# A planned MoE, recurrence and MoE kernel: row normalisation moved from VectorE to GpSimd between its scatters, the pauses taken out, first groups of 4, 4 and 8 units

## What is computed

```python
x = x + 0.5 * ffn(layernorm(x))      # 8 experts, 128 -> 512 -> 128, relu squared; each token uses the expert of its largest router logit
x = x + rnn(layernorm(x))            # h = tanh(Wi x_t + bi + bh + Wh h), 512 steps, all 16 sequences at once
x = x + 0.5 * ffn(layernorm(x))      # the same experts again
```

## Time and profile before

| what | value |
|---|---|
| median of 3 executions | 612.68 us (606.79 to 624.44) |
| the profiled execution | 603.88 us, span 602.0 us |
| TensorE busy | 551.4 us (92%) |
| VectorE busy | 412.8 us (69%) |
| GpSimd busy | 423.5 us (70%), of which 187 pauses 116.0 us |
| ScalarE busy | 315.4 us (52%) |
| indirect DMAs of GpSimd | 64 + 64 scatters, 64 gathers, 71 puts, each 984 to 988 ns on average |
| normalisations on VectorE | 192 of 128x128, 65.1 us in all |

### The profile page before, as it was taken

The page is one execution under the profiler, slowest core; times in us unless marked ns, Lnnn a source line. Parts: engine busy times, 40 slices in busy tenths (PEclk is TensorE's granted clock), DMA queues, the critical chain, the costliest instruction groups (busy, mean ns, idle before and its releaser), DMA issues.

```text
span 602.0 us, 16237 instructions
## 1 busy us (share of the span) xinstructions
PE 551.4 (92%) x4714; PEld 533.7 (89%) x4714; DVE 412.8 (69%) x1507; ACT 315.4 (52%) x1089; POOL 423.5 (70%) x520
## 2 busy tenths in 40 slices
PE   7799798997999989999999999998999999869991
PEld 6798698897999989999999999997889999658991
DVE  5789867886667878657876774577546466665661
ACT  2133165464666546666666666654346666425660
POOL 2699497789995778978874987838849638664552
PEclk9889999998999999999999999999999999998997
DMA  5977432221222223322321532101152301435310
GB/s 184 296 273 289 109 105 81 79 78 59 78 80 69 66 82 97 93 68 63 98 81 49 132 111 77 39 27 68 45 144 76 84 20 69 139 115 151 101 37 1
DMA packets 54163, 58.89 MB, mean 98 GB/s; under 512 B 8999, under 2 KB 42034, under 8 KB 54080
## 3 DMA queue, kind: packets, MB, share of 16 engines
q1 hardware_dynamic: 44064, 36.68, 21.0%
q0 software_dynamic: 9440, 21.06, 10.8%
q10 hardware_dynamic: 576, 0.13, 0.1%
HBM read 27.67 MB, written 30.62 MB: 97 GB/s over the span
## 4 chain that ended last, share of the span: by engine, by line
PE 74%; DVE 11%; issue 7%; DMA 2%; SPq 1%; ACT 1%; another core or an unknown queue 1%; ACTq 0%; POOLq 0%; DVEq 0%
PE yp L1687 23%; PE hp L1677 20%; PE z L1697 11%; PE mT L1583 4%; PE lg L1627 3%; PE xTp L1666 3%; PE hp L1702 3%; DMA hsT<-in_L_attn_x_dram 2%; PE z L1647 2%; PE yp L1707 2%; DVE pay L1238 2%; DVE r_sb L1361 2%; PE hp L1616 1%; SPq L1012 1%
## 5 line engine op out<-in xcount | busy, mean ns | idle before, releaser
L1687 PE MATMUL yp<-projT,s_sb 128*128 x1248 | 198.3, 291 | 11.6 <-ACT s_sb L1495 5.9
L1677 PE MATMUL hp<-xT_sb,w_sb 128*128 128x128 f32 x1248 | 193.2, 286 | 2.0 <-DVE xT_sb L1355 1.3
L1687 PEld LDWEIGHTS yp<-projT,s_sb 128*128 128x128 f32 x1248 | 161.3, 194 | 14.6 <-issue 14.2
L1466 ACT ACTIVATE hsT<-z 128x16 f32<-128x16 f32 x512 | 93.5, 183 | 147.5 <-PE z L1697 102.7
L1677 PEld LDWEIGHTS hp<-xT_sb,w_sb 128*128 128x128 f32 x1248 | 161.7, 193 | 3.1 <-DVE xT_sb L1355 1.4
L1697 PEld LDWEIGHTS z<-hsT,wT 128*128 128x128 f32 x1024 | 154.0, 190 | 8.9 <-ACT hsT L1466 3.0
L1697 PE MATMUL z<-hsT,wT 128*128 128x16 f32 x1024 | 158.0, 230 | 1.4 <-ACT hsT L1466 1.2
L1495 ACT ACTIVATE s_sb<-r_sb 128x256 f32<-128x256 f32 (+1 forms) x252 | 115.7, 461 | 74.5 <-issue 51.8
L1361 DVE TENSOR_SCALAR r_sb<-hp 128x512 f32<-128x512 f32 x156 | 106.9, 686 | 66.6 <-PE hp L1677 55.9
L1152 POOL MEMSET idle<- 128x600 f32 x187 | 116.0, 620 | 0.2
L1189 POOL DMA_INDIRECT out_dram<-y_sb,xs_sb x71 | 70.1, 988 | 61.7 <-DVE y_sb L1368 34.9
(11 more groups left out here) (132 smaller groups left out, 564.3 us busy)
## 6 DMA issues: line engine op xcount, KB each, us to landing
xs_sb<-xs_dram SPq DMA_DIRECT2D x71, 129.0 KB
xs_sb<-xy_dram SPq DMA_DIRECT2D x85, 64.0 KB
xy_dram<-y_sb SPq DMA_DIRECT2D x85, 64.0 KB
xy_dram<-zeros SPq DMA_DIRECT2D x10, 512.0 KB, 6.0
hsT<-in_L_attn_x_dram SPq DMA_DIRECT2D x16, 256.0 KB
hsT<-n_L_ffn_expert_proj_dram SPq DMA_DIRECT2D x2, 1024.0 KB
fc_sb<-in_L_ffn_expert_fc_dram SPq DMA_DIRECT2D x1, 2048.0 KB
out_dram<-y_sb,xs_sb POOLq DMA_INDIRECT x71
```

Of the source, the lines that this page charges most:

```text
L1466: act.activation(state(t), z_step(t), ACT.Tanh).then_inc(s_h, 1)
L1677: mm = pe.matmul(hp[:, g % 2, h * P:(h + 1) * P], w_sb[:, g % 2, h * P:(h + 1) * P], xT_sb[:, g % 2, :], start=True, stop=True)
L1687: mm = pe.matmul(yp[:, 0:D], s_sb[:, g % 2, h, :], projT[:, bass.ds(offsets[g] + h * D, D)], start=(h == 0), stop=(h == HC - 1))
```

## The change

The normalisation of the two expert layers goes from VectorE to GpSimd. There it stands row tile by row tile between the scatters: the row tile j+1 is normalised ahead of the scatter of row tile j. The normalisation ahead of the recurrence stays on VectorE. The pauses are gone everywhere. The first layer's groups are 4, 4 and 8 units instead of 5, 3 and 8, the second layer's 4, 3, 2, 3, 2, 1, 1 instead of 3, 2, 2, 3, 2, 2, 1, 1, and the weights of the planner are others. Two of the first four units are loaded by ScalarE's DMA queue instead of SyncE's. The lists padded per expert are 23, 23 and 39 tiles, 85 as before. In the new plan GpSimd also takes the root of the second group in the middle of the first group's scatters, after nine of sixteen. And the gathers of unit 0 stand after four scatters of the third group, with the other early gathers mixed among these scatters; before, 31 of the 32 scatters of the third group stood in one row between the gathers of unit 2 and those of unit 3.

```diff
-FIRST = [5, 3, 8]
-STEP = [1, 3, 1]
-MIDDLE = [1, 1, 1, 1, 1, 1, 1, 1, 1, 1, 3, 3]
-SECOND = [3, 2, 2, 3, 2, 2, 1, 1]
+FIRST = [4, 4, 8]
+STEP = [1, 2, 1]
+MIDDLE = [1, 1, 1, 1, 1, 1, 2, 1, 1, 1, 3, 1, 1]
+SECOND = [4, 3, 2, 3, 2, 1, 1]
...
-REST = 600
+REST = 0
+PACE = 1.75
...
-PR = {'proj': -38.387, 'lat1': 30.338, 'lat2': 69.811, 'lat3': -18.484, 'last': 24.985,
+PR = {'proj': 82.557, 'lat1': 204.589, 'lat2': 80.915, 'lat3': -54.818, 'last': -288.677,
...
-AHEAD = [4, 5, 7]
+AHEAD = [3, 6, 7]
...
-    ROW, LAND, WINDOW = 1.27 + REST / 900, 2.2, 3.413
+    ROW, LAND, WINDOW = PACE if REST else 1.35, 2.2, 3.413
+    NORM = 0.45
...
     def normalising(r):
         n = range(r.J // 4)
-        return [("stats", r, i) for i in n] + [("root", r)] + [("norm", r, i) for i in n]
+        return [("stats", r, i) for i in n] + [("root", r)]
...
+            if what == "scatter" and p[1][2] + 1 < key.J:
+                pool_order.append(("norm", key, p[1][2] + 1))
+                start += NORM
+            while REST and drained > start + PR["burst"]:
+                pool_order.append(("rest",))
+                start += REST / 1250
+            pool_order.append(p[1])
+            pool_free, drained = start + 1.27, max(drained, start) + PACE
...
+        def by_act(u):
+
+            return u < FIRST[0] and u % 2 == 1
...
+            def normalise_row(r, j):
+
+                n, w = r.n0 + j, int(r.second)
+                if j == 0:
+                    pool.wait_ge(s_root, root_no["root", r.index])
+                pool.tensor_scalar(pay[:, n, XN:XN + D], row_in(w, n), mv[:, w, n, 0:1], rstd[:, w, n:n + 1],
+                                   ALU.subtract, ALU.mult).then_inc(s_row, 1)
+
             rests = [0]
...
-                if j % 4 == 0:
-                    pool.wait_ge(s_norm, 4 * norm_no["norm", r.index, j // 4])
+                pool.wait_ge(s_row, row_no[r.index, j])
...
-            def normalise(what, c, i):
-                w = 2 if what == "mnorm" else int(c.second)
-                dve.wait_ge(s_root, root_no["mroot" if what == "mnorm" else "root", c.index])
-                for n in range(c.n0 + 4 * i, c.n0 + 4 * i + 4):
-                    dve.tensor_scalar(pay[:, n, XN:XN + D], row_in(w, n), mv[:, w, n, 0:1], rstd[:, w, n:n + 1],
+            def normalise(m, i):
+                dve.wait_ge(s_root, root_no["mroot", m.index])
+                for n in range(m.n0 + 4 * i, m.n0 + 4 * i + 4):
+                    dve.tensor_scalar(pay[:, n, XN:XN + D], row_in(2, n), mv[:, 2, n, 0:1], rstd[:, 2, n:n + 1],
                                       ALU.subtract, ALU.mult).then_inc(s_norm, 1)
...
+            for u in range(min(FIRST[0], NU // 2)):
+                if by_act(u):
+                    act.dma_start(raw(u), x[:, u * UNIT:(u + 1) * UNIT, :].rearrange("b (th j) d -> th b (j d)", j=UR)
+                                  ).then_inc(s_in[u], 16)
```

More of the change, by code:

```diff
@@ L136, in first_in @@
         else:
-            at += {"rows": 1.1, "proj": 4.0, "fc": 8.0}[what[0]]
+            at += {"rows": 1.3, "proj": 4.0, "fc": 8.0}[what[0]]
         arrive[what] = at + 2.0
@@ L232, in urgency @@
         what = job[1][0][0]
-        return 16.0 - pe + PR["proj"] if what == "proj" else spare(job[0]) + (what in ("stats", "root", "norm")) * PR["late"]
+        return 16.0 - pe + PR["proj"] if what == "proj" else spare(job[0]) + (what in ("stats", "root")) * PR["late"]
     def pool_urgency(p):
@@ L757, in plan @@
             r = p[1] if len(p) > 1 else None
-            if p[0] == "place" or p[0] == "norm" and p[2] == r.J // 4 - 1:
-                placed, normed = ("place", r), ("norm", r, r.J // 4 - 1)
-                if placed in ev and normed in ev and r not in sorted_out:
-                    sorted_out.add(r)
-                    for j in range(r.J):
-                        pool_wait.append((max(ev[placed], ev["norm", r, j // 4], 0.0 if r.second else ev.get(("clean", r.index), 0.0)),
-                                          ("scatter", r, j)))
+            if p[0] == "place":
+                for j in range(r.J):
+                    pool_wait.append((max(ev[p], 0.0 if r.second else ev.get(("clean", r.index), 0.0)), ("scatter", r, j)))
             if p[0] == "list" and p[2] == 0 and r.last:
@@ L1073, in _ @@
                 if what[0] == "rows":
-                    rows_in(what[1])
+                    if not by_act(what[1]):
+                        rows_in(what[1])
                 elif what[0] == "zero":
@@ L1418, in side @@
                     statistics(*piece)
-                elif what in ("norm", "mnorm"):
-                    normalise(*piece)
+                elif what == "mnorm":
+                    normalise(*piece[1:])
                 elif what == "pick":
```

57 lines of the change are left out of this document (30 added, 27 removed).

## The result

The changed kernel takes 698.66 us (median of four runs, 691.60 to 706.73); the kernel before, on the same chip, takes 609.85 us. The ratio is 1.143, with a 95% interval of 1.133 to 1.153: clearly slower, where 588 us and 4.1% faster were predicted, and far above the range of 574 to 612 us. The profiled execution takes 691.87 us, its span is 689.8 us.

What follows compares the result with a forecast made beforehand. Bound taken: start 69.8 us, TensorE's work 494.4, holes 26.4, tail 11.4. Start -11.4, work -11.3 and holes -2 turn 603.9 into 579.2 us profiled, 588 us as a median (-4.1%), range 574 to 612 us.

Steps and rivals of the forecast that it cites:

- The pauses: GpSimd: 187 pauses of 0.61 us go, indirect DMAs follow one another in 1.27 us; their lack was priced at nothing.
- indirect DMAs that take longer than 0.97 us: Sign named as what would make all of the forecast wrong, if they do so once they follow closely.
- The normalisation: One row tile on GpSimd: taken as 0.45 us, between 0.29 and 0.55, giving a scatter spacing of 1.59 us (1.43 to 1.69).
- 20 us of slack: Third group: GpSimd's last early scatter ends near 162 us, while TensorE wants the group's first tile near 185 us.
- The start: Up to the first expert product: 58.4 us instead of 69.8, so -11.4 us, between -15 and -6.
- The rival of the start: The start gains nothing, by slow normalisation or a long wait at the root: 601 us as a median; chance 0.17.
- TensorE's work: From the first expert product on: 64 filler records go (13.3 us), the third group's rank adds 2.05 us; -11.3 us.
- The holes: TensorE's idle time after the first expert product: -2 us, between -8 and +12, as VectorE no longer normalises the third group.
- The rival of the dense order: Late gathers and scatters make TensorE stand still, then run at half clock; five holes give 623 us median; chance 0.13.
- The port lock: GpSimd's normalisations delay VectorE through shared ports, 6.3 us on the chain: 594 us as a median; chance 0.12.
- the sum: Whole kernel: 603.9 - 11.4 - 11.3 - 2 = 579.2 us profiled, times 1.0146 for the median.

Runs made afterwards that it cites:

- e6: The changed kernel, its order word for word, with 121 pauses of 0.62 us ahead of gathers and output transfers directly behind another indirect transfer: ratio 1.034.
- e5: The kernel before, its order word for word and VectorE normalising as before, with only GpSimd's pauses left out: 828 us, 36% slower.
- e1: The changed kernel, same order, with GpSimd normalising only 32 of a row's 128 columns: only about 10 us came back.
- e9: The changed kernel's order with pauses put in and GpSimd normalising only 32 of 128 columns: 590.8 us, 3.7% under the kernel before.
- e11: The changed kernel without pauses, its gathers and indirect transfers to the output moving 64 instead of 128 columns a row: the changed kernel's ratio.
- e14: The changed kernel's order with pauses ahead of gathers only, transfers to the output following each other without one: ratio 1.040.

## Why the prediction was wrong, step by step

**The pauses: the step that failed.** "So I price the lack of pauses at nothing". In the order of the change they are worth 10.9 points of the ratio (e6), near 66 us, in the old one 36% (e5). The step rested on one row, the scatter at 519.60 us that kept its 0.96 us without pauses. The row is right and shows the wrong thing: the transfer isn't slower, the engines that wait for TensorE's signals are. And the sign was there in the kernel before, on the other engines beside this very row. GpSimd issues bare transfers 1.27 us apart from 517.06 us on; these are VectorE's rows, and the stretches behind the second (columns as above):

```profile
524.30 0.69 DVE L1361 TENSOR_SCALAR r_sb<-hp 128x512 f32<-128x512 f32 x1 [2.64 <-remote]
...
540.10 0.29 DVE L1368 SCALAR_TENSOR_TENSOR y_sb<-yp,xs_sb 128x128 f32<-128x128 f32 x1 [3.40 <-remote]
```
```profile
539.00:543.00 4.00, 1.59 (x12) 1.15 (x10) 1.53 (x6) 0.91 (x2) 2.03 (x3) 1.00 0.35 118
543.00:547.00 4.00, 3.99 (x18) 3.50 (x19) 2.03 (x5) 1.79 (x3) 0.97 (x1) 0.57 0.59 133
```

Seven of the eight signals that come over 0.8 us late in the kernel before lie between 520 and 544 us, where GpSimd doesn't pause. What I had named as the proof against me, "indirect DMAs that take longer than 0.97 us", never came: bare gathers take 0.94 to 0.95 us in the stretch shown.

**The normalisation: mis-sized.** 0.82 us measured, 0.45 taken, and 0.55 the upper end. The extrapolation from 4 and 32 columns used an operation with an immediate in place of the two 128x1 operands; e1 gives 0.50 us at 32 columns with two operands of 128x1, so 0.0033 us a column and 0.39 us before the first. With the scatter's 1.07 us the spacing became 2.1 to 2.3 us, above the 1.69 us I had as the worst. With the pauses in place this is worth 36.5 us (e6 to e9, medians); in the profiled executions 19.6 of 33.1 us are idle time of TensorE. "20 us of slack" for them were not there.

**The start: half right.** The first scatter was to start at 20.7 us and starts at 20.73. No wait stands at the root (2.4 us taken), its 2.96 us are as said. But the last scatter of the first group starts at 56.55 us instead of 50.9: the fifteen spacings took some 7.7 us more than forecast, and the wait that didn't come gave 2.4 back. And the first expert product at 63.4 instead of 58.4: -6.4 us, where -11.4 was predicted and -6 was the end of the range. The rival of the start put its limit at 0.91 us for a normalisation, and 0.82 us plus the 0.10 us by which the scatter is dearer come to it; that the start still gains is owed to the wait that stayed away.

**TensorE's work: right in kind, and more than forecast.** -11.3 us predicted, -15.4 us at full clock measured, and the same in e6 and e9 (476.8 and 476.5 us).

**The holes: -2 us (to +12) predicted, +36.6 us of idle time and 73.0 us by the clock measured.** The rival of the dense order had the form right: idle stretches, then a clock of 0.5, a hole of 3 us costing 3 + 4 us. It missed the size: 29 gaps of 1 us and more in the changed kernel, 62 us together, and 16 stretches of half clock with 181 us, where the kernel before has 12 gaps, 20 us together, and 17 us of half clock (each without the stretch at the end). And it missed the cause. It looked for rows that arrive late; only 4.5 us of GpSimd's and 5.4 us of TensorE's waits ended in a transfer that landed, while the engines that need no row stood still.

**The port lock** was a rival with 0.12. Its sign was that VectorE's operations with two inputs get longer beside normalisations, and they do, by little. This operation over 99 columns takes 0.26 us beside nothing and beside pauses; here it began 0.12 us after a normalisation:

```profile
174.63 0.80 POOL L1163 TENSOR_SCALAR pay<-hsT,mv,rstd 128x128 f32<-128x128 f32 x1
```
```profile
174.75 0.43 DVE L1338 TENSOR_TENSOR inside<-inside,change 128x99 f32<-128x99 f32 x1
```

The rule of the Trainium skill cited in the prediction (SBUF — State Buffer, "Who interferes with whom") agrees with this row, and with the pauses, beside which the same operation keeps its 0.26 us. What was drawn from it doesn't follow. The row at 28.82 us that was to show it is of an operation with one input, held by a pause that only writes, so it is no case of the rule on two inputs. Over the whole program, by an estimate from the traces (each operation against the time that its like takes undisturbed), VectorE's two-input operations (TENSOR_TENSOR) are 5.5 us longer in the changed kernel, 1.3 us in the kernel before. All its others are 11.7 us longer, where they were 43.5 us with the pauses, 5.4 us in e5 without them. So the two-input operations lost about 4 us and VectorE as a whole gained. The 1.3 us by which the rule was to make the start later rest on no row, and the first scatter is where the sum without them put it. The lock is not the cause of the loss: ScalarE, which shares no port in that rule, is late as much as VectorE. The same section also says "DMA never contends with a compute engine". The data of a DMA don't here: e11 moves half of them and nothing changes. But closely issued indirect transfers of GpSimd do hold others up, in these runs by up to 19.79 us.

**That the two errors make up the forecast's miss** is what e9 shows. With the pauses, and a normalisation near the price that I took (0.50 us, by leaving out three quarters of it), the kernel takes 590.8 us; the sum gave 588. That they lie within 3 us is in part luck: the sum gave 579.2 us for the profiled execution, which takes 587.4, and the factor of 1.0146, taken from the kernel before, made up for most of it (e9's median is only 1.006 times its profiled execution).

## What to carry to other kernels

An operation that computes nothing can be what keeps the machine running: before a pause is priced at nothing, run the kernel without it, and look at the engines beside it rather than at the one that pauses. Where GpSimd issues many indirect transfers, watch for waits with the releaser "remote" and for tanh, relu or copies that start late after their input; here a spacing 0.3 us shorter costs 8%, and one 0.7 us longer 13%. And a new operation in a tight chain is measured in its own form, with its own operands, before its price goes into an order.

## What the runs showed of the hardware

- Behind indirect transfers that GpSimd issues 1.25 us apart, signals of TensorE reach ScalarE and VectorE 1 to 18 us after the recorded end of the product, and the waiting instruction starts 0.02 us after the signal (46 signals over 0.8 us late in the changed kernel, 76 in e5, five in e6). At 1.74 us apart almost none is late, at 1.45 us most of it is still there (13 of the 23 tanh behind four transfers). DMA engines are 14 to 37% busy meanwhile. The number of bytes plays no part (e11). Close issuing alone isn't enough (e14 has it between transfers to the output, and no late signal). Whether the product itself ends late or only its signal is late stays open: the ends of products are modelled in these profiles. So does the path by which GpSimd's transfers do it.
- A GpSimd TENSOR_SCALAR with two 128x1 operands takes 0.50 us for 128x32 and 0.82 us for 128x128; VectorE does four of 128x128 in 1.11 us. An indirect DMA issued right behind one takes 1.07 us, behind a memset 0.97.
- Memsets of 600 columns on GpSimd held VectorE's one-input operations: an operation of 11 columns takes 0.17 us alone and 0.65 us beside one (28.82 us in the kernel before).
- The 16 stretches in which the granted clock of the changed kernel was 0.5 (3 to 24 us each, 1.2 GHz instead of 2.4) came after idle time of TensorE: the one from 58.6 us on behind a gap of 5.4 us, the one from 130.2 us on behind a gap of 3.9 us.
